# A four-layer attention and FFN program on one core: reordering the DMA queue of the first attention

## What is computed

```python
def _L0_xattn_ref(q, k, v):        # q: layernorm(x), k = v: context; b = 64, d = 64, m = 256
    h = 8
    qh = q.reshape(b * h, d // h, m)
    kh = k.reshape(b * h, d // h, -1)
    vh = v.reshape(b * h, c // h, -1)
    scale = 1.0 / jnp.sqrt(jnp.asarray(d // h, dtype=q.dtype))
    qk = jnp.einsum('bdm,bdn->bmn', qh, kh) * scale
    sm = jax.nn.softmax(qk, axis=-1)
    ret = jnp.einsum('bmn,bcn->bcm', sm, vh)
    return ret.reshape(b, c, m)
x = x + _L0_xattn_ref(_layernorm(x, axis=-1), ctx_2048, ctx_2048)
```

## Time and profile before

| | |
|---|---|
| median of 3 launches | 2517.65 us (2515.28 to 2520.46) |
| the profiled launch, its own time | 2522.49 us |
| its span, first to last instruction | 2520.6 us |
| mean granted TensorE clock | 0.792 |
| first attention, PE's first to last unit start | 146.6 to 570.0 us |
| busy over the span: PE, DVE, ACT, POOL | 1518.6, 1622.3, 1062.1, 613.7 us |

### The profile page before, as it was taken

The page is one execution under the profiler, slowest core; times in us unless marked ns, Lnnn a source line. Parts: engine busy times, 40 slices in busy tenths (PEclk is TensorE's granted clock), DMA queues, the critical chain, the costliest instruction groups (busy, mean ns, idle before and its releaser), DMA issues. The chain is left out here.

```text
span 2520.6 us, 34997 instructions
## 1 busy us (share of the span) xinstructions
PE 1518.6 (60%) x11260; PEld 924.7 (37%) x11260; DVE 1622.3 (64%) x3141; ACT 1062.1 (42%) x1453; POOL 613.7 (24%) x862
## 2 busy tenths in 40 slices
PE   1069999994995787874334343279999367620022
PEld 1035555552774544542112112135555233310011
DVE  6457777773453477675777887445555487856787
ACT  4427667673221334344355455323333377710022
POOL 4312233332002223223333433201010011105500
PEclk9999999996998788897555556689999688855555
DMA  6635555542001221211000000001100100003001
GB/s 179 173 77 117 119 120 119 119 114 76 1 0 30 51 60 40 47 43 56 10 1 1 0 0 0 21 29 31 29 25 23 51 1 0 1 21 61 6 26 41
DMA packets 94652, 120.97 MB, mean 48 GB/s; under 512 B 25868, under 2 KB 78284, under 8 KB 89932
## 3 DMA queue, kind: packets, MB, share of 16 engines
q1 hardware_dynamic: 94540, 119.56, 19.0%
HBM read 79.75 MB, written 22.09 MB: 40 GB/s over the span
## 5 line engine op out<-in xcount | busy, mean ns | idle before, releaser
L571 DVE TENSOR_REDUCE ratt_nmax<-ratt_psS 128x2 f32<-128x512 f32 x512 | 319.9, 684 | 112.6 <-PE ratt_psS L463 112.0
L537 ACT ACTIVATE ratt_E<-ratt_psT 128x1024 f32<-128x1024 f32 x256 | 255.6, 1022 | 123.9 <-PE ratt_psT L485 123.8
L463 PE MATMUL ratt_psS<-ratt_K,ratt_Q 72*128 72x256 bf16 x1024 | 210.7, 291 | 54.4 <-DMA ratt_K<-ratt_ones 48.5
L485 PE MATMUL ratt_psT<-ratt_Q,ratt_K 75*128 75x256 bf16 x1024 | 202.6, 283 | 15.2 <-DMA ratt_Q<-ratt_rows 14.8
L498 PE MATMUL ratt_psO<-ratt_E,ratt_V 128*32 128x256 f32 x2048 | 144.8, 403 | 0.7 <-ACT ratt_E L537 0.7
L463 PEld LDWEIGHTS ratt_psS<-ratt_K,ratt_Q 72*128 72x128 bf16 x1024 | 82.3, 101 | 154.2 <-issue 94.0
L1833 PE MATMUL nffn_psH<-nffn_W,nffn_QT 128*128 128x512 bf16 x128 | 57.7, 601 | 114.6 <-DVE nffn_H L1797 95.8
L485 PEld LDWEIGHTS ratt_psT<-ratt_Q,ratt_K 75*128 75x128 bf16 x1024 | 102.4, 101 | 36.2 <-issue 16.8
L1316 PE MATMUL gatt_psA<-gatt_DA,gatt_same 128*128 128x512 f32 x128 | 89.1, 786 | 25.3 <-DVE gatt_DB L1201 25.3
L1135 POOL TENSOR_TENSOR gatt_DA<-gatt_own,gatt_a 128x1024 f32<-128x1024 f32 x32 | 61.5, 1935 | 143.4 <-PE gatt_psA L1319 90.4
L1756 POOL TENSOR_TENSOR nffn_H<-nffn_H,nffn_gam 128x1024 f32<-128x1024 f32 x32 | 93.1, 2937 | 7.4 <-DVE nffn_H L1788 7.4
(11 more groups left out here) (451 smaller groups left out, 4124.3 us busy)
## 6 DMA issues: line engine op xcount, KB each, us to landing
ratt_Q<-z_parts SPq DMA_DIRECT2D x32, 576.0 KB
ratt_K<-context_parts SPq DMA_DIRECT2D x96, 192.0 KB
gatt_V<-in_ctx_dram SPq DMA_DIRECT2D x16, 512.0 KB, 6.9
z_parts<-prep_ZS SPq DMA_DIRECT2D x48, 128.0 KB, 2.7
context_parts<-prep_CS SPq DMA_DIRECT2D x48, 128.0 KB
head_sums<-ratt_O SPq DMA_DIRECT2D x64, 72.0 KB
all_X<-in_x_dram SPq DMA_DIRECT2D x8, 512.0 KB, 4.8
prep_C<-in_ctx_dram SPq DMA_DIRECT2D x8, 512.0 KB, 5.6
```

Source lines behind the costliest of these rows:

```text
L463: mm = nc.tensor.matmul(psS[:, RING[h], c * D:(c + 1) * D], Q9[0:R, buf, h, k % 2, c * P:(c + 1) * P], K9[0:R, buf, h, k % 2, :], start=Tr ...
L485: mm = nc.tensor.matmul(psT[:, p % 2, e, c, :], K9[0:RM, buf, h, u, c * P:(c + 1) * P], Q9[0:RM, buf, h, u, :], start=True, stop=True)
L537: nc.scalar.activation(E[:, 2 * b + p // 2, 2 * (p % 2):2 * (p % 2) + 2], psT[:, p % 2], ACT.Exp, scale=SCALE).then_inc(exped, 1)
L571: nc.vector.tensor_reduce(nmax[:, k % 2, h, :], psS[:, RING[h]].rearrange("p (c t) -> p c t", c=2), AX.X, ALU.max, negate=True).then_inc(m ...
```

## The change

It does five things, all in `row_attention`:

1. On SP, the row of maxima comes first in every slot; loads follow it.
2. Q and K are loaded in different slots: Q in odd slots, three ahead as before; the same group's K in the next, even slot, two ahead.
3. `inverses_out` moves from slots 4j+3 to 4j+4, in front of `out`. `back` moves from slots 4j+4 to 4j+6, behind that slot's row and K load. `out` and `sums_back` keep their slots, behind row and load. On DVE the reciprocal moves from slots 4j+2 to 4j+3; on POOL the scaling moves from slots 4j+5 to 4j+7.
4. The four DMAs of ones are issued ahead of the first four loads and no longer between them.
5. The tail is one or two slots longer on three engines.

The core of the diff:

```diff
                 def slot(i, k):
                     n = i * 8 + k
-                    row_there = held(sp, n) if is_unit(n - 1) else None
-                    if k % 2 == 1 and past(n, 5) and is_unit(n + 3):
-                        free = held(sp, n * 4 - 4 * LAG)
-                        pair = held(sp, i * 2 + (k + 3) // 4)
-                        sp.wait_ge(shifted, free)
-                        load(pair, (k + 3) // 2 % 2, (k + 3) // 2 % BUFS)
...
+                    if is_unit(n - 1):
+                        bring_row(held(sp, n), (k - 1) // 2 % BUFS, (k - 1) % 2)
+                    if past(n, 5):
+                        g = (k + 3) // 2 if k % 2 else (k + 2) // 2
+                        if is_pair(i * 2 + g // 2):
+                            if k % 2:
+                                free, pair = held(sp, n * 4 - 4 * LAG), held(sp, i * 2 + g // 2)
+                                sp.wait_ge(shifted, free)
+                                load_q(pair, g % 2, g % BUFS)
+                            else:
+                                load_k(held(sp, i * 2 + g // 2), g % 2, g % BUFS)
                     c = (k - 8) // 4
...
+                    if k % 4 == 0 and is_pair(i * 2 + c - 1):
+                        inverses_out(held(sp, (i * 2 + c - 1) * P), held(sp, i * 2 + c), (c - 1) % 2)
+                    if k % 4 == 0 and is_pair(i * 2 + c):
+                        out(held(sp, i * 2 + c), held(sp, (i * 2 + c) * 4 + 4), c % 2)
+                    if k % 4 == 1 and is_pair(i * 2 + c):
+                        sums_back(held(sp, (i * 2 + c) * 16), c % 2, held(sp, (i + c // 2) * 64 + 64))
+                    if k % 4 == 2 and is_pair(i * 2 + c - 1):
+                        back(held(sp, (i * 2 + c - 1) * 16), (c - 1) % 2, held(sp, (i + (c - 1) // 2) * 16 + 16))
...
-                    load(buf // 2, buf % 2, buf)
-                slots(sp, slot, UNITS + 9)
+                for g in range(BUFS):
+                    load_q(g // 2, g % 2, g)
+                    load_k(g // 2, g % 2, g)
+                slots(sp, slot, UNITS + 11)
...
-                    c = (k - 13) // 4
-                    if k % 4 == 1 and is_pair(i * 2 + c):
+                    c = (k - 15) // 4
+                    if k % 4 == 3 and is_pair(i * 2 + c):
                         scale_and_add(i * 2 + c, c % 2, i + c // 2)
...
-                    c = (k - 10) // 4
-                    if k % 4 == 2 and is_pair(i * 2 + c):
+                    c = (k - 11) // 4
+                    if k % 4 == 3 and is_pair(i * 2 + c):
                         dve.wait_ge(d_in[c % 2], (i + c // 2) * 16 + 16)
```

More of the change, by code:

```diff
@@ L319, in _, with load_q, load_k @@
             def _(sp):
-                def load(pair, b, buf):
+                def load_q(pair, b, buf):
                     q = zq.rearrange("s r a (b h) u m -> (s r) a b (h u m)", b=2)[:, bass.ds(pair, 1), b, :]
-                    k = ck.rearrange("r s a (b h) u m -> (r s) a b (h u m)", b=2)[:, bass.ds(pair, 1), b, :]
                     sp.dma_start(Q9[0:R, buf].rearrange("p h u m -> p (h u m)"), spread(
                         q.rearrange("p a m -> p (a m)"), 1, 3)).then_inc(group_in[buf], 16)
+                def load_k(pair, b, buf):
+                    k = ck.rearrange("r s a (b h) u m -> (r s) a b (h u m)", b=2)[:, bass.ds(pair, 1), b, :]
                     for part in range(3):
@@ L361, in slot @@
                     n = i * 8 + k
-                    row_there = held(sp, n) if is_unit(n - 1) else None
-                    if k % 2 == 1 and past(n, 5) and is_unit(n + 3):
-                        free = held(sp, n * 4 - 4 * LAG)
-                        pair = held(sp, i * 2 + (k + 3) // 4)
-                        sp.wait_ge(shifted, free)
-                        load(pair, (k + 3) // 2 % 2, (k + 3) // 2 % BUFS)
-                    ago = k % 4
-                    c = (k - 8) // 4
[L370 to L386, removed]
@@ L387, in slot @@
-                    if row_there is not None:
-                        bring_row(row_there, (k - 1) // 2 % BUFS, (k - 1) % 2)
+                    if is_unit(n - 1):
[9 more added lines that the diff above has]
+                                load_k(held(sp, i * 2 + g // 2), g % 2, g % BUFS)
@@ L441, in slot @@
                         split_max(n - 1, (k - 1) % 2)
-                    c = (k - 13) // 4
-                    if k % 4 == 1 and is_pair(i * 2 + c):
+                    c = (k - 15) // 4
+                    if k % 4 == 3 and is_pair(i * 2 + c):
                         scale_and_add(i * 2 + c, c % 2, i + c // 2)
-                slots(pool, slot, UNITS + 10)
+                slots(pool, slot, UNITS + 12)
             @block.tensor
@@ L582, in _ @@
                 nc.vector.tensor_copy(identb[:], ident[:]).then_inc(ident_set, 1)
-                slots(dve, slot, UNITS + 7)
+                slots(dve, slot, UNITS + 8)
 def pipeline(engine, front, back):
```

## The result

The change makes the kernel slower by about half a per cent: 2529.06 us (2521.24 to 2534.89, six launches) against 2516.47 (2509.44 to 2520.46, six launches), a ratio of 1.0048 with a 95% interval of 1.0029 to 1.0068. That is 12 us, in an interval of 7 to 17. The profiled launch of the changed kernel took 2523.67 us, with a span of 2521.8.

The account below looks back on a forecast made before the run. PE's own work bounds the kernel, at 6.19 us a steady slot, plus 31.9 us in long slots. Terms -31.9 + 8 + 54 - 6.5 + 1 = +24.6 gave 2547 or 2542.2 us; put down 2541, range 2532 to 2552 (chance 0.5).

Parts of the forecast that it names:

- six long slots: Slots where PE waits for a late row of maxima: 14.8 us of waits, 31.9 us with what follows, expected to go.
- Part 1: SP's queue, row of maxima first: the six waits of PE go, with their clock, -31.9 us.
- Part 2: K loaded one slot later: PE waits 0.5 us for K at 16 loads, +8 us (3 to 10).
- formula of the Trainium skill: DMA time of about 2.0 us plus bytes at 436 GB/s: K lands 3.4 us after issue, no stall, sum 2480.
- Part 3: Results later: POOL's scaling waits for `num`, its split is late, PE stalls 2.8 us; 12 x 4.5 = +54 us.
- rival that the clock stays up: No clock fall behind PE's stalls: 12 x 3.3 = 40 in place of 54, 2528 us; chance 0.22.
- rival with longer falls: Clock low for more than a slot after each stall, each costing 6 us or more: 2560 us; chance 0.1.
- floor of 3.3 us: Least cost of a PE stall if the clock stayed: late row and K behind it make two slots 3.3 us longer.
- transfer: Time `den` and `num` still need after K has landed: 1.9 us, between 0 and 2.4.
- first rival: `den` and `num` come at the latest 1.9 us before K's landing, so no stall: 2494 us; chance 0.09.
- Part 4: Stage start, ones first: PE's first multiplication with maxima starts near 155 instead of 161.74 us, -6.5 us.
- Part 5: Stage end: `back` of the pair before stands ahead of the last inverses, +1 us (0 to 3).

Follow-up runs that it names:

- e: The changed kernel with K right behind Q in odd slots and POOL's scaling two slots later: 2479.39 us, 0.9866 of the kernel before.
- b: The changed kernel with POOL's scaling two slots later still, nothing on SP changed: 2488.78 us, 0.989 of the kernel before.
- g: The kernel before with only the row of maxima first in every slot: 2623.71 us, 1.0431 of the kernel before.
- f: The changed kernel with PE filling the stall with 18 transposes whose result is overwritten: 2509.25 us, 0.9972 of the kernel before.
- a: The kernel before with only the four DMAs of ones ahead of the first loads: 2507.38 us, 0.997 of the kernel before.
- third launch: The changed kernel unchanged, profiled a third time: excess over 58 steady slots 44.0 us.
- c: The changed kernel with K right behind Q in odd slots again, row still first: 2499.60 us, 0.9927 of the kernel before.
- d: The changed kernel with `back` ahead of the row and the K load of its slot: 2495.43 us, 0.9919 of the kernel before.

## Why the prediction was right in direction and wrong in size

**What bounded the kernel** was read rightly. e shows that the stage is PE's work once no one is late, and b that the six long slots of the earlier trace rows do go. One reading of the rows was off without consequence: what stands behind a full load lands 9.8 us after the load began (491.20 to 501.01), not 9.6.

**Part 1** was entered as -31.9 us. In the three launches before, the excess is 29.8 on average, so the term was 2 us too large; one launch is not the mean. It was right only in company: g shows that the row first alone costs 109 us.

**Part 2**, K one slot later: forecast 0.5 us each and +8; measured 0.4 each and 4.4 us in all (b). Where PE waited, K landed about as forecast (6.0 us after its issue in the slot shown under b; I had 6.1), but in b only 12 of the 28 loads made PE wait: slot 48 of the changed kernel starts in time, 5.56 us after K's issue at 460.67. The formula of the Trainium skill in the prediction, which gives 3.4 us, is fitted there to DMAs that GpSimd issues; those here are SyncE's, and K took 6.0.

**Part 3 is the step that failed**, by size and in its clock term above all: 2.2 us for a clock fall behind every one of 12 stalls, 26 us, where the runs show 14.4. The mechanism, the stall, held. Part 3 was 12 x 4.5 = 54 us, made of 2.8 for the stall, 2.2 for the clock and -0.5. With part 2 it was 62; measured are 44.1. Term by term:

| term, 12 stalls | forecast | measured | shown by |
|---|---|---|---|
| stall less what PE gets back | 2.3 each, 28 us | some 2.1 each, 25 us | slot 48; the excess of f, less K waits |
| clock | 2.2 each, 26 us | 14.4 us | f against the changed kernel |
| K waits | 8 us | 4.4 us | b |

The clock is the largest; f, which sizes it, is one profiled launch, and the times of f put it at 18 to 19 us, still under 26. The prediction took a fall behind each stall, because all six long slots of its one launch had one (two of them in the earlier trace rows). The clock fell behind four or five of twelve, and where it did, stall and fall cost 3.5 to 6.7 us, 5.7 on average of the first launch's five, where 4.5 stood in the sum. The rival that the clock stays up gave 2528 us, almost the time that was measured, but that is no proof of it: it held for seven of twelve stalls, and K, the stall and the start were off as well. The rival with longer falls, 6 us or more for each stall, held for three of the other five (6.4 to 6.7 us). Nor was there the floor of 3.3 us for a stall without a fall; 2.16 us were measured, and no K wait followed in slot 50. The K load behind the late row went out at phase 8.6 of its slot, and had 5.9 us to land before S(50), counted from 474.85 to 480.77.

The **transfer** term of 1.9 us stood behind a K landing at 12.9; the scaling began at 14.0 in place of 14.8. That explains the half microsecond that the stall is shorter, and the first rival's condition, results 1.9 us earlier, was not near.

**Part 4** was too small, -6.5 us for about -11. The row at the start, columns as above:

```profile
131.78 3.17 PE L460 MATMUL ratt_psS<-ratt_K,ratt_Q 72*128 72x256 bf16 x12 [33.83 <-DMA ratt_K<-context_parts]
...
140.60 6.42 SPq L334 DMA_DIRECT2D ratt_Q<-ratt_rows  x4
...
152.49 0.61 PE L482 MATMUL ratt_psT<-ratt_Q,ratt_K 75*128 75x256 bf16 x2 [5.36 <-DMA ratt_Q<-ratt_rows]
```

The mechanism held: PE starts 15 us earlier and then waits for a row that was issued at 140.60 and stands behind the four loads. But the row landed by 152.5 (150.0 and 152.6 in the other two launches) and not near 155. The loads' bytes end a little behind 151, where the rate has dropped to 22 GB/s (117 in the microsecond before, 0 in the next):

```profile
151.00:152.00 1.00, 0.00 (x0) 0.00 (x0) 0.00 (x0) 0.00 (x0) 0.00 (x0) 1.00 0.12 22
```

I had them end at 151.7, with 2 to 3 us more for landing; from the last byte to PE's start it took 1 to 1.5. The 11 us are the difference of S(5) between profiles; the launches with part 4 alone (a) gave 7, and their interval has room for both sizes.

**Part 5**: the last `den` goes out at 605.65, 33.6 us after S(63) = 572.09, against 31.5 before (601.48 and 570.0), so +2.1 us for +1. The changed kernel's row, and the next stage's first DMA, which stood at 609.33 before:

```profile
605.65 0.54 SPq L358 DMA_DIRECT2D ratt_den<-inverse_sums  x1
...
613.57 0.42 SPq L708 DMA_DIRECT2D sffn_W<-in_L_ffn_w_dram  x1
```

In the third launch the clock fell there too, and the next stage began at 618.1 us.

**The sum again**, with means of three launches: +14.3 in the stretch, -11.1 at the start, +2 to +4 at the end, some +5 to +7 us for the stage; the next stage's first DMA goes out 7.3 us later in the mean (606.7 and 613.9). The spans of the profiled launches agree (2517.6 before, 2522.1 after, means of three), while the launches without a profile differ by 9 to 13 us (ratios 1.0045 and 1.0048). These 5 us or so stay open. The stages behind this one differ by 3 to 4 us from launch to launch of one kernel in the profiles, and a profile shows one launch at a time, so I can't say where they lie. Why the clock fell at all six long slots before, in each of three launches, and at fewer than half of the stalls after isn't settled either. It isn't the length alone: the waits before are a little longer on average, 14.8 us for six against 27.9 for thirteen, but the first of the six was only 1.4 to 1.6 us in the three launches and had a fall each time, and c and d had falls behind waits as short.

The Trainium skill, TensorE: Matmul & The Clock Gate, section What's actually happening, says that the same kernel can show different numbers of slow matmuls at its start from one run to the next. It speaks of the first matmuls and not of falls in the middle; the traces here show the like in the middle: falls behind five, four and five of twelve like stalls, mostly different ones.

## What to carry to other kernels

When a queue's order is changed, follow each moved DMA to the in-order engine that waits for it, and ask what stands behind that wait: here a wait of 6.5 us for something that nobody needed soon cost nothing itself, and 38 us, the clock's part included, through the split queued behind it. The mend was to move the waiting instruction, not the DMA. And a stall on a tensor engine at its limit has two prices, the stall and a clock fall that comes only sometimes: count the falls over several launches before giving each stall one, or fill the stall.

## What the runs showed of the hardware that I had not expected

- 1.17 us of useless transposes in a stall of 2.3 us kept the granted clock at 1.00 for 388.7 us and gained 14.4 us (f), although PE still waited about 1.1 us each time (14.8 us, 13 times).
- Stalls of about the same length, in the same place of the program, once in four slots, had a fall behind them in some cases and none in others: 2.08 us with, 2.27 us without, within one launch.
- In d, whose waits are for K at a slot's start, the clock fell behind a wait of 1.19 us; twelve stalls of 1.8 to 2.5 us in the changed kernel had no more than five falls in any of three launches.
- `den` and `num` behind half a load landed 1.0 us (`num`) and 1.3 us (`den`, 3.5 to 4.8) later in the median than with nothing of size in front. From issue to landing in the kernel before, then in the changed one, for `num` (least, median, most):

```profile
DMA to landing us min/median/max: 3.6/3.8/5.0
```

```profile
DMA to landing us min/median/max: 3.7/4.8/5.5
```
